# The second chunk of a tile's transposes behind the step's first job instead of in front of it

## Chip, core and metric

The kernel runs on 1 core of one Trainium2 chip. The metric is device time in microseconds (us) of one execution, given as the median of several. Lower is better.

## What is computed

x is 2 x 1024 tokens of 256 numbers. The result is x + attention(norm(x)) + ffn(norm(x)).

```python
x = L0_attn_x
xn = _layernorm(x, axis=-1)
x = x + _L0_attn_ref(xn, Wq, bq, Wk, bk, Wv, bv, Wo, bo) + _L0_ffn_ref(xn, gate, up, down, ...)

# attention: b, t = 2, 1024; 16 heads of 128
q = (x @ Wq + bq).reshape(b, h, t, dh)
k = (x @ Wk + bk).reshape(b, t, h, dh).transpose(0, 2, 3, 1)
v = (x @ Wv + bv).reshape(b, t, h, dh).transpose(0, 2, 1, 3)
logits = jnp.einsum('bhtd,bhds->bhts', q, k) * scale
weights = jax.nn.softmax(logits + mask, axis=-1)        # causal mask
out = jnp.einsum('bhts,bhsd->bhtd', weights, v)
return out.transpose(0, 2, 1, 3).reshape(b, t, h * dh) @ Wo + bo
```

The feed-forward part (4-bit weights, a gelu gate) runs in the first 320 us of the kernel and isn't touched.

## The kernel before

There are 2 x 16 = 32 heads, numbered 0 to 31, one after the other. Each has 8 query tiles of 128 rows, so the attention is a sequence of 256 steps; step s = 8h + i is position i of head h. In heads 0 to 30 tile i stands at position i; head 31 takes its tiles in the order 4, 6, 7, 5, 2, 3, 1, 0. Tile t looks at t + 1 key blocks of 128.

Every product is computed in three fp32r pieces (`split_matmul`, L41, L42, L43), each value being split into a high and a low part. A tile passes through all engines:

- PE: `scores(s)`, queries times keys, into one of two pairs of PSUM banks S.
- DVE L963: negative maximum and copy to `probs`. ACT L507: exp. POOL L737, L740: the reciprocal of the row sum and the product with it; this ends in `probs_done`.
- PE: three steps later (LAG = 3), `transposes(s - LAG)`: t + 1 transposes of 128 x 128 (L1169). Tiles 4 to 7 have two chunks: key blocks 0 to 3, and the rest (1, 2, 3 or 4 blocks). The chunks of all tiles go in turn into two PSUM banks T. The first transpose of a chunk waits on `pt_lo_done` until the chunk before the last one has been copied out of its bank.
- ACT L493 (`pt_high`): copy of a chunk out of its bank into `pt_hi`. DVE L880 (`pt_low`): the remainder into `pt_lo`, which frees the bank.
- PE: `with_v`, products with the values.

Between these stand jobs of six or twelve products: K (keys of a head, `project_k`), V (values, `project_v`) and O (a quarter of the output product, `output`). A table by position says which job stands where: FIRST is between the transposes and the scores of the step, EARLY behind the scores, LATE behind `with_v`. A job waits for `job_lo_done` of the job before it, since they share the bank M. A K or V job is copied out by ACT (L472, L475) and then by DVE (L835, L839), an O job by DVE alone (L846).

```python
EVEN = {0: {EARLY: "K0"}, 1: {FIRST: "K1"}, 2: {EARLY: "O0a"}, 3: {LATE: "O0b"}, 4: {EARLY: "V0", LATE: "V1"},
        6: {FIRST: "O1a"}, 7: {FIRST: "O1b"}}
ODD = {0: {EARLY: "V2"}, 1: {FIRST: "K1"}, 2: {EARLY: "V3"}, 3: {LATE: "O0a"}, 4: {EARLY: "O0b", LATE: "K0"},
       6: {FIRST: "O1a"}, 7: {FIRST: "O1b"}}
```

Head 0 has no first job; head 1 is as ODD from position 1 on; head 30 is as EVEN, with O1a and O1b early and one more early K job at position 5; head 31 has first jobs at positions 1 (V3), 2 (O0a), 4 (O1a) and 5 (O1b). In heads 7, 15 and 23 steps of the Q projection (`q_step`) stand behind positions 1, 2, 4 and 5 as well.

The order of each engine is the order of its code. ACT's step is: `pt_high(s - LAG)` for both chunks, then `evacuate` of the first job, then exp, then the early job. DVE's step is: `pt_low` of both chunks, the first job's copy, the maximum of step s, the early job's copy.

Of the kernel before, what the change touches and what calls it, by code (L numbers as in the profile page):

```python
# [38 lines left out]
def split_matmul(nc, out, w_hi, w_lo, m_hi, m_lo, start, stop):  # L39

    nc.tensor.matmul(out, w_hi, m_hi, start=start, stop=False)  # L41
    nc.tensor.matmul(out, w_hi, m_lo, start=False, stop=False)  # L42
    return nc.tensor.matmul(out, w_lo, m_hi, start=False, stop=stop)  # L43


def wait(eng, sem, count):

    if count > 0:
        eng.wait_ge(sem, count)
# [6 lines left out]
def attention(nc, sh, d, out):  # L56
# [8 lines left out]
    LAG = 3  # L65
# [15 lines left out]
    with ExitStack() as c:  # L81
# [103 lines left out]
        def job_of(h, i, where):  # L185

            name = JOBS[h].get(i, {}).get(where)
            if name is None:
                return None
            if name[0] == "K":  # L190
                return ("K", h if name == "K1" else h + 1, int(name[1]))
            if name[0] == "V":
                return ("V", h // 2, int(name[1]))
            return ("O", h - 1, int(name[1]), "ab".index(name[2]))
# [10 lines left out]
        banks_of = lambda i: 1 if i < QT else 2  # L205
# [9 lines left out]
        def k_of(h, half):  # L215

            if half and h + 1 == NH:
                return [t[:, 0:N] for t in wq_space]
            return [t[:] for t in (k_right if half else (k_even, k_odd)[h % 2])]

        def q_of(h, half):

            if half and h + 1 == NH:
                return [t[:, N:2 * N] for t in wq_space]
            return [t[:, half, :] for t in (q_hi, q_lo)]
# [57 lines left out]
        def freed_by(job):  # L283

            if job in (END[1], END[3], ("K", 0, 1), ("V", 0, 1)):
                return 0
            return max((nth[other] for other in ORDER[:nth[job] - 1] if (other in elsewhere) == (job in elsewhere)), default=0)
# [705 lines left out]
        def _(pe):  # L993
            def bank_free(*turn):

                if place[turn] < 2:
                    return
                kind, a, b = TURNS[place[turn] - 2]
                if kind == "S":
                    pe.wait_ge(max_done, step_of(a, b) + 1)  # L1000
                elif kind == "F":
                    pe.wait_ge(hid_done, a + 1)
                else:
                    pe.wait_ge(q_even_done, a * GROUP + b + 1)
                    pe.wait_ge(q_odd_done, a * GROUP + b + 1)
# [44 lines left out]
            def down(p, b):  # L1050

                pe.wait_ge(hid_lo_done, 2 * p + 2)
                if p == 0:
                    pe.wait_ge(xt_lo_done, KC * TC)
                if p:
                    pe.wait_ge(acc_done, half_no(p - 1, b))
                for t in range(2):
                    cols = slice((2 * b + t) * P, (2 * b + t + 1) * P)
                    for k in (2 * p, 2 * p + 1):
                        slot = slot_of(chunk_j(k))  # L1060
                        last = split_matmul(nc, D[b][:, t * DM:(t + 1) * DM], hid_hi[:, k % 4, cols], hid_lo[:, k % 4, cols],
                                            w_hi[:, slot, 4 * P:W6], w_lo[:, slot, 4 * P:W6], k == 2 * p, k == 2 * p + 1)
                last.then_inc(down_done, 1)
# [38 lines left out]
            def run(job):  # L1102
                if job is None:
                    return
                wait(pe, job_lo_done, freed_by(job))
                last = {"K": project_k, "V": project_v, "O": output}[job[0]](*job[1:])
                if job != END[3]:
                    last.then_inc(job_done, 1)

            def q_step(o, u):  # L1110
                bank_free("Q", o, u)
                cols = slice(o * N, (o + 1) * N)
                for v in range(2):
                    n = o * HEADS + 2 * u + v
                    pe.wait_ge(wq_lo_done, n + 1)
                    for ch in range(KC):
                        last = split_matmul(nc, bank_of("Q", o, u)[:, v, :], wq_hi[:, n % LOADS, ch, :],
                                            wq_lo[:, n % LOADS, ch, :], xn_hi[:, ch, cols], xn_lo[:, ch, cols],
                                            ch == 0, ch == KC - 1)
                    last.then_inc(qp_done, 1)  # L1120
# [17 lines left out]
            def scores(s):  # L1138
                h, i = divmod(s, TILES)
                tile = tile_of(h, i)  # L1140
                bank_free("S", h, tile)
                if i == 0:
                    pe.wait_ge(job_lo_done, nth[("K", h, 0)])
                if tile == QT:
                    pe.wait_ge(job_lo_done, nth[("K", h, 1)])
                half, cols = tile // QT, slice(tile % QT * P, (tile % QT + 1) * P)
                if i == 0 or half != tile_of(h, i - 1) // QT:
                    pe.wait_ge(q_lo_done, q_count(h, half))
                hi, lo = q_of(h, half)
                for bank in range(half + 1):  # L1150
                    width = min(N, (tile + 1) * P - bank * N)
                    keys_hi, keys_lo = k_of(h, bank)
                    last = split_matmul(nc, bank_of("S", h, tile)[:, bank, 0:width], hi[:, cols], lo[:, cols],
                                        keys_hi[:, 0:width], keys_lo[:, 0:width], True, True)
                last.then_inc(scores_done, 1)

            def transposes(s):
                i = tile_at(s)
                pe.wait_ge(probs_done, s + 1)
                if s == 0:  # L1160
                    pe.wait_ge(acc_done, STEPS)
                if s == 1:
                    pe.wait_ge(job_lo_done, nth[("K", 0, 1)])
                for ch in range(banks_of(i)):
                    at = chunk_no(s, ch)
                    wait(pe, pt_lo_done, at - 1)
                    for n in range(min(QT, i + 1 - ch * QT)):
                        b = ch * QT + n
                        last = nc.tensor.transpose(T[at % 2][:, n * P:(n + 1) * P], probs(s, i)[:, b * P:(b + 1) * P],  # L1169
                                                   ident[:])  # L1170
                    last.then_inc(pt_done, 1)

            def with_v(h, m, side):

                last_tile = QT * m + QT - 1
                blocks = range(QT) if side == "left" else range(QT, TILES)
                pe.wait_ge(pt_lo_done, chunk_no(step_of(h, last_tile), blocks[-1] // QT) + 1)
                pe.wait_ge(job_lo_done, nth[("V", h // 2, blocks[-1] // 2)])
                if blocks[0] == 0:
                    wait(pe, o_lo_done, 2 * h + m if h + 1 < NH else 2 * h)  # L1180
                for b in blocks:
                    first = max(b - QT * m, 0) * P
                    last = split_matmul(nc, O[:, first:], v_hi[:, h % 2, b, :], v_lo[:, h % 2, b, :],
                                        pt_keys(pt_hi, m, b), pt_keys(pt_lo, m, b), b == 0, b == last_tile)
                if blocks[-1] == last_tile:
                    last.then_inc(pv_done, 1)
# [50 lines left out]
            for s in range(NH * TILES):  # L1237
                h, i = divmod(s, TILES)
                if s >= LAG:
                    transposes(s - LAG)  # L1240
                run(job_of(h, i, FIRST))
                scores(s)
                run(job_of(h, i, EARLY))
                if s == 1:
                    down(*halves_at(STEPS + 1))
                    down(*halves_at(STEPS + 2))
                for m, side in pv_at(h, i):
                    with_v(h - 1, m, side)
                run(job_of(h, i, LATE))
                for u in q_steps(h, i):  # L1250
                    q_step(h // GROUP + 1, u)

            end = NH * TILES
            with_v(NH - 1, 1, "left")
            transposes(end - 3)
            transposes(end - 2)
            with_v(NH - 1, 1, "right")
            transposes(end - 1)
# [53 lines left out]
```

## Time and profile before

| | before |
|---|---|
| median of 3 runs | 1227.37 us (1227.34 to 1227.98) |
| the profiled execution | 1227.42 us, of which the trace spans 1225.6 us |
| PE busy | 1213.0 us (99%), 7556 products |
| DVE busy | 855.2 us (70%) |
| ACT busy | 746.7 us (61%) |
| POOL busy | 747.3 us (61%) |
| PE clock granted | 1.0 over the span |

A product's row starts when the product before it has been streamed, and its own duration reaches over the start of the next; the distance between two starts is what a product costs in the stream. PEld is PE's loading of stationary operands, which runs ahead of the products.

### The profile page before, as it was taken

Reading aid. Unit: us, or ns where it says so; the run is one execution under the profiler, and the core shown is the slowest. Engines: PE = TensorE matmul, PEld = TensorE weight load, DVE = VectorE, ACT = ScalarE, POOL = GpSimd, SP = SyncE. Lnnn points to the kernel's source line nnn. Section 1 sums busy time; section 2 is a strip of 40 time slices with the busy share of each in tenths; the row PEclk is TensorE's granted clock in tenths of the full one; section 3 lists DMA queues with packets and bytes.
Section 4 is the critical chain, followed back from the end, with each engine's and each line's share of the span. In section 5 each row is a group of like instructions: output and inputs, shape, how many; then the busy total and the mean of one; then the engine's idle time right before and its main releaser. Section 6 shows DMA issues by size and latency. Waiting matters only on the chain.

```text
span 1225.6 us, 20582 instructions
## 1 busy us (share of the span) xinstructions
PE 1213.0 (99%) x7556; PEld 1077.0 (88%) x7556; DVE 855.2 (70%) x1675; ACT 746.7 (61%) x1548; POOL 747.3 (61%) x797
## 2 busy tenths in 40 slices
PE   9999999999999999999999999999999999999998
PEld 7788888888889899889899988889898889899987
DVE  6777777776676766766677666676767766677675
ACT  5644444444576766666666765676667666666664
POOL 7346455543677666536767772677667536767764
PEclk9999999999999999999999999999999999999999
DMA  7100000000000000110000012010000100000001
GB/s 170 32 7 14 14 12 8 27 1 9 14 13 14 14 21 27 44 31 14 27 14 14 14 31 65 14 48 14 14 27 23 56 1 13 27 14 14 14 6 35
DMA packets 57347, 29.86 MB, mean 24 GB/s; under 512 B 16289, under 2 KB 57249, under 8 KB 57249
## 3 DMA queue, kind: packets, MB, share of 16 engines
q1 hardware_dynamic: 55888, 27.49, 8.0%
q8 instruction: 62, 1.02, 0.3%
q10 hardware_dynamic: 1360, 1.06, 0.3%
q14 instruction: 37, 0.30, 0.1%
HBM read 26.44 MB, written 2.10 MB: 23 GB/s over the span
## 4 chain that ended last, share of the span: by engine, by line
PE 93%; DVE 3%; ACT 2%; DMA 1%; POOL 1%; issue 1%; SPq 0%; DVEq 0%; ACTq 0%; POOLq 0%
PE ps L41 27%; PE ps L43 27%; PE ps L42 27%; PE ps L1169 10%; PE ps L1031 1%; DMA wq_in<-in_wq 1%; DVE pt_lo L880 1%; ACT q_all L415 0%; DVE acc L846 0%; DVE probs L963 0%; DMA acc<-in_x 0%; ACT wq_hi L405 0%; ACT pt_hi L493 0%; POOL wq_lo L624 0%; SPq L325 0%
## 5 line engine op out<-in xcount | busy, mean ns | idle before, releaser
L740 POOL TENSOR_TENSOR probs<-probs,inv_sum 128x128 f32<-128x128 f32 (+7 forms) x256 | 293.6, 1147 | 20.1
L737 POOL TENSOR_TENSOR inv_sum<-row_sum,minus_one 128x1 f32<-128x1 f32 x256 | 140.5, 549 | 219.5 <-ACT probs L507 218.4
L507 ACT ACTIVATE probs<-probs,neg_max 128x128 f32<-128x128 f32 (+7 forms) x256 | 198.8, 777 | 92.9 <-DVE neg_max L963 90.4
L493 ACT ACTIVATE pt_hi<-ps 128x512 fp32r<-128x512 f32 (+3 forms) x384 | 173.5, 488 | 91.4 <-PE ps L1169 88.7
L880 DVE TENSOR_TENSOR pt_lo<-ps,pt_hi 128x512 fp32r<-128x512 f32 (+3 forms) x384 | 200.6, 550 | 15.9 <-ACT pt_hi L493 15.8
L963 DVE CUSTOM_DVE_ANT_0 probs<-ps,mask_row 128x128 f32<-128x128 f32 (+7 forms) x256 | 191.8, 749 | 6.6
L1169 PE MATMUL ps<-ident,probs 128*128 128x128 f32 x1152 | 168.7, 274 | 3.2 <-DVE pt_lo L880 1.8
L721 POOL TENSOR_TENSOR hid_lo<-act_buf,hid_hi 128x512 fp32r<-128x512 f32 x64 | 82.8, 1294 | 139.5 <-ACT hid_hi L447 139.5
L1169 PEld LDWEIGHTS ps<-ident,probs 128*128 128x128 f32 x1152 | 133.8, 141 | 16.1 <-issue 5.2
L42 PE MATMUL ps<-pt_lo,v_hi 128*128 128x512 f32 (+3 forms) x386 | 133.0, 344 | 0.0
L43 PE MATMUL ps<-pt_hi,v_lo 128*128 128x512 f32 (+3 forms) x386 | 132.9, 344 | 0.0
L41 PE MATMUL ps<-pt_hi,v_hi 128*128 128x512 f32 (+3 forms) x386 | 130.2, 337 | 0.0
L846 DVE TENSOR_TENSOR acc<-ps,acc 128x512 f32<-128x512 f32 x127 | 86.9, 685 | 57.9 <-PE ps L43 57.9
L624 POOL TENSOR_TENSOR q_lo<-q_all,q_hi 128x512 fp32r<-128x512 f32 x63 | 81.3, 1291 | 73.5 <-ACT q_hi L484 73.5
L548 ACT ACTIVATE act_buf<-ps 128x512 f32<-128x512 f32 x64 | 38.2, 597 | 132.2 <-PE ps L43 132.2
L41 PE MATMUL ps<-xn_hi,w_hi 128*128 128x512 f32 x256 | 102.9, 402 | 1.1 <-DVE act_buf L933 1.1
L42 PE MATMUL ps<-xn_lo,w_hi 128*128 128x512 f32 x256 | 101.3, 396 | 0.0
L43 PE MATMUL ps<-xn_hi,w_lo 128*128 128x512 f32 x256 | 101.0, 394 | 0.0
L888 DVE SCALAR_TENSOR_TENSOR o_lo<-ps,bv,o_hi 128x512 fp32r<-128x512 f32 x63 | 47.3, 751 | 74.6 <-ACT o_hi L500 74.6
L839 DVE TENSOR_TENSOR v_lo<-ps,v_hi 128x512 fp32r<-128x512 f32 x64 | 44.2, 691 | 59.2 <-ACT v_hi L475 59.2
L41 PEld LDWEIGHTS ps<-pt_hi,v_hi 128*128 128x128 f32 x386 | 72.5, 188 | 8.8
L42 PEld LDWEIGHTS ps<-pt_lo,v_hi 128*128 128x128 f32 x386 | 72.6, 188 | 8.7
(154 smaller groups left out, 3372.4 us busy)
## 6 DMA issues: line engine op xcount, KB each, us to landing
wq_in<-in_wq SPq DMA_DIRECT2D x63, 128.0 KB, 2.3
kv_in<-in_wk SPq DMA_DIRECT2D x16, 256.0 KB, 2.6
wo_in<-in_wo SPq DMA_DIRECT2D x32, 128.0 KB, 2.0
kv_in<-in_wv SPq DMA_DIRECT2D x32, 128.0 KB, 2.4
out<-acc SPq DMA_DIRECT2D x7, 256.0 KB, 2.8
acc<-in_x SPq DMA_DIRECT2D x2, 512.0 KB, 5.3
raw<-in_gate SPq DMA_DIRECT2D x16, 64.0 KB, 1.8
raw<-in_up SPq DMA_DIRECT2D x16, 64.0 KB, 2.1
```

The costliest lines, as they stand in the source:

```text
L41: nc.tensor.matmul(out, w_hi, m_hi, start=start, stop=False)
L42: nc.tensor.matmul(out, w_hi, m_lo, start=False, stop=False)
L43: return nc.tensor.matmul(out, w_lo, m_hi, start=False, stop=stop)
L493: nc.scalar.activation(pt_blocks(pt_hi, i, ch), T[at % 2][:, 0:blocks * P].rearrange("p (a b) -> p a b", b=P), ACT.Copy).then_inc(pt_hi_do ...
L507: nc.scalar.activation(row, row, ACT.Exp, bias=neg_max[:, s % 16:s % 16 + 1], scale=-1.0, accum_out=row_sum[:, s % 16:s % 16 + 1]).then_in ...
L721: nc.gpsimd.tensor_tensor(hid_lo[:, k % 4, :], act_buf[:, k % 4, :], hid_hi[:, k % 4, :].bitcast(F32), ALU.subtract).then_inc(hid_lo_done, 1)
L737: nc.gpsimd.tensor_tensor(inv_sum[:, at], row_sum[:, at], minus_one[:], ALU.pow).then_inc(inv_done, 1)
L740: nc.gpsimd.tensor_tensor(row, row, inv_sum[:, at].to_broadcast([P, (tile_of(h, i) + 1) * P]), ALU.mult).then_inc(probs_done, 1)
L846: ins = nc.vector.tensor_tensor(sums, bank_for(job), sums, ALU.add)
L880: nc.vector.tensor_tensor(pt_blocks(pt_lo, i, ch), T[at % 2][:, 0:blocks * P].rearrange("p (a b) -> p a b", b=P), pt_blocks(pt_hi, i, ch). ...
L963: nc.vector.tensor_tensor_reduce(probs(s, tile), flat(bank_of("S", h, tile))[:, 0:width], mask_row[:, SEQ - width:SEQ], -1.0, -MASKED, ALU ...
L1169: last = nc.tensor.transpose(T[at % 2][:, n * P:(n + 1) * P], probs(s, i)[:, b * P:(b + 1) * P], ident[:])
```

## The change

`transposes` takes the chunks to do. In every step the first chunk stands where both stood; the second now stands behind the first job and in front of the scores. Nothing else is edited: the code of ACT, DVE, POOL and the DMA queues is the same.

```diff
-            def transposes(s):
+            def transposes(s, chunks=(0, 1)):
                 i = tile_at(s)
                 pe.wait_ge(probs_done, s + 1)
...
-                for ch in range(banks_of(i)):
+                for ch in chunks[:banks_of(i)] if 0 in chunks else chunks[:banks_of(i) - 1]:
...
                 if s >= LAG:
-                    transposes(s - LAG)
+                    transposes(s - LAG, (0,))
                 run(job_of(h, i, FIRST))
+                if s >= LAG:
+                    transposes(s - LAG, (1,))
                 scores(s)
```

The order moves where a step has a first job and the tile of three steps ago has two chunks: position 1 of heads 1 to 30 (tile 6, 4 + 3 transposes around K1), position 7 of heads 1 to 29 (tile 4, 4 + 1 around O1b), and positions 1, 2, 4 and 5 of head 31: 63 places. The wait for `probs_done` is now written twice in each of 253 steps.

On PE, position 1 of head 2, before (the names with `kv_` are job K1, those with `k_` and `q_` the scores):

```order
L1169 MATMUL ps<-ident,probs 128x128 x7
L41 MATMUL ps<-xn_hi,kv_hi 128x512
L42 MATMUL ps<-xn_lo,kv_hi 128x512
L43 MATMUL ps<-xn_hi,kv_lo 128x512
L41 MATMUL ps<-xn_hi,kv_hi 128x512
L42 MATMUL ps<-xn_lo,kv_hi 128x512
L43 MATMUL ps<-xn_hi,kv_lo 128x512
L41 MATMUL ps<-k_hi_even,q_hi 128x256
```

and with the change:

```order
L1169 MATMUL ps<-ident,probs 128x128 x4
L41 MATMUL ps<-xn_hi,kv_hi 128x512
L42 MATMUL ps<-xn_lo,kv_hi 128x512
L43 MATMUL ps<-xn_hi,kv_lo 128x512
L41 MATMUL ps<-xn_hi,kv_hi 128x512
L42 MATMUL ps<-xn_lo,kv_hi 128x512
L43 MATMUL ps<-xn_hi,kv_lo 128x512
L1169 MATMUL ps<-ident,probs 128x128 x3
L41 MATMUL ps<-k_hi_even,q_hi 128x256
```

Three of the seven transposes of tile 6 have moved behind the six products of K1.

On ACT, positions 1 and 2 with the change (`k_hi_right` is the copy of K1):

```order
L493 ACTIVATE pt_hi<-ps 128x4x128
L493 ACTIVATE pt_hi<-ps 128x3x128
L472 ACTIVATE k_hi_right<-ps,bk 128x512
L493 ACTIVATE pt_hi<-ps 128x4x128 x2
L507 ACTIVATE probs,row_sum<-probs,neg_max 128x256
```

Nothing has moved here: the copy of the three-block chunk stands ahead of the copy of K1, as before, and so it does on DVE. At position 7 one of the five transposes of tile 4 moves in the same way, behind the six products of O1b.

## Rows read from the trace of the kernel before

**Rows 1.** The page, busy time and share of the span by engine

```profile
PE 1213.0 (99%) x7556; PEld 1077.0 (88%) x7556; DVE 855.2 (70%) x1675; ACT 746.7 (61%) x1548; POOL 747.3 (61%) x797
```

**Rows 2.** Timeline of DVE, head 10: start us, us, instruction [idle before <-releaser]

```profile
600.85 0.55 DVE L880 TENSOR_TENSOR pt_lo<-ps,pt_hi 128x384 fp32r<-128x384 f32 x1
601.76 0.75 DVE L835 SCALAR_TENSOR_TENSOR k_lo_right<-ps,bk,k_hi_right 128x512 fp32r<-128x512 f32 x1 [0.36 <-ACT k_hi_right L472]
602.77 0.69 DVE L880 TENSOR_TENSOR pt_lo<-ps,pt_hi 128x512 fp32r<-128x512 f32 x1
```

**Rows 3.** Timeline of PEld, head 10, positions 2 and 3

```profile
601.52 0.14 PEld L1169 LDWEIGHTS ps<-ident,probs 128*128 128x128 f32 x1
602.57 0.19 PEld L41 LDWEIGHTS ps<-wo_hi,o_hi 128*128 128x128 f32 x1
603.57 0.14 PEld L1169 LDWEIGHTS ps<-ident,probs 128*128 128x128 f32 x1 [0.24 <-issue]
```

**Rows 4.** PEld, first load of the position-2 job: heads 2 and 30

```profile
373.20 0.19 PEld L41 LDWEIGHTS ps<-wo_hi,o_hi 128*128 128x128 f32 x1
...
1164.60 0.19 PEld L41 LDWEIGHTS ps<-wo_hi,o_hi 128*128 128x128 f32 x1
```

**Rows 5.** Timeline of ACT, head 10, positions 1 and 2

```profile
599.93 0.49 ACT L493 ACTIVATE pt_hi<-ps 128x384 fp32r<-128x384 f32 x1
601.04 0.69 ACT L472 ACTIVATE k_hi_right<-ps,bk 128x512 fp32r<-128x512 f32 x1 [0.62 <-PE ps L43]
601.83 1.08 ACT L493 ACTIVATE pt_hi<-ps 128x512 fp32r<-128x512 f32 x2
```

**Rows 6.** Timeline of PE, head 10, positions 1 to 3

```profile
598.66 0.95 PE L1169 MATMUL ps<-ident,probs 128*128 128x128 f32 x7
599.37 0.47 PE L41 MATMUL ps<-xn_hi,kv_hi 128*128 128x512 f32 x1
...
600.84 0.28 PE L41 MATMUL ps<-k_hi_even,q_hi 128*128 128x256 f32 x1
...
601.19 1.03 PE L1169 MATMUL ps<-ident,probs 128*128 128x128 f32 x8
601.98 0.42 PE L41 MATMUL ps<-k_hi_even,q_hi 128*128 128x384 f32 x1
...
602.59 0.36 PE L41 MATMUL ps<-wo_hi,o_hi 128*128 128x256 f32 x1
602.79 0.28 PE L42 MATMUL ps<-wo_lo,o_hi 128*128 128x256 f32 x1
...
603.60 0.30 PE L1169 MATMUL ps<-ident,probs 128*128 128x128 f32 x1
```

**Rows 7.** Copy of O1a on DVE, then first load of O1b: heads 9, 10

```profile
591.49 0.68 DVE L846 TENSOR_TENSOR acc<-ps,acc 128x512 f32<-128x512 f32 x1
592.22 0.19 PEld L41 LDWEIGHTS ps<-wo_hi,o_hi 128*128 128x128 f32 x1
...
617.27 0.68 DVE L846 TENSOR_TENSOR acc<-ps,acc 128x512 f32<-128x512 f32 x1
618.09 0.19 PEld L41 LDWEIGHTS ps<-wo_hi,o_hi 128*128 128x128 f32 x1
```

**Rows 8.** Head 9 into 10: tile 5's probs on POOL, its first transpose's load

```profile
592.73 1.47 POOL L740 TENSOR_TENSOR probs<-probs,inv_sum 128x768 f32<-128x768 f32 x1
594.25 0.14 PEld L1169 LDWEIGHTS ps<-ident,probs 128*128 128x128 f32 x1
```

**Rows 9.** Head 31: loads that end PE's waits, and what DVE did

```profile
1195.06 0.68 DVE L846 TENSOR_TENSOR acc<-ps,acc 128x512 f32<-128x512 f32 x1
1195.79 0.19 PEld L41 LDWEIGHTS ps<-wo_hi,o_hi 128*128 128x128 f32 x1 [0.50 <-DVE acc L846]
```

**Rows 10.** Timeline of PE, head 10, position 4

```profile
607.90 0.38 PE L1169 MATMUL ps<-ident,probs 128*128 128x128 f32 x2
608.04 0.48 PE L41 MATMUL ps<-k_hi_even,q_hi 128*128 128x512 f32 x1
```

## The prediction

> **What bounds the kernel.** I read the page's shares first: PE is busy 99% of the span [rows 1]. So nothing that makes another engine faster can gain much, but anything that lets PE wait is lost one for one. The question is then how much spare time the waits of PE have at the places where the order moves. For that I took the timelines of all engines at positions 1 and 2 of a head, and there the reader should see three things.
>
> First, the bank of a chunk. The second chunk of tile 7 (position 2) goes into the bank of the second chunk of tile 6 (position 1). DVE has emptied that bank at 600.85 + 0.55 = 601.40 [rows 2], and PE starts the load for the next chunk at 601.52 [rows 3]. PE didn't wait there, but the smallest distance of such a load behind such a copy that I see is 0.12: the transpose at 603.57 does wait, idle for 0.24, for the copy 602.77 + 0.69 = 603.46 [rows 2, 3]. So the margin is about nothing.
>
> Second, the bank of the jobs. The load of the job at position 2 starts at 602.57, 0.06 behind the end of K1's copy, 601.76 + 0.75 = 602.51 [rows 2, 3]. It is held by this copy already. The same 0.06 (0.053 unrounded) stands in 26 heads, from the load at 373.20 in head 2 to that at 1164.60 in head 30 [rows 4]; heads 7, 15 and 23 aren't among them, for two steps of the Q projection stand between.
>
> Third, ACT waits 0.62 for PE before it copies K1, at 601.04 [rows 5]. Its copy of the three-block chunk is long done (599.93 + 0.49). With the change this copy can't start until K1 is done, and K1's own copy still stands behind it.
>
> **Position 1, worked out on head 10.** PE does the same 4 + 6 + 3 instructions, so it loses nothing by itself. Transposes start 0.11 apart and the next product 0.03 behind the last one: eight take 601.98 - 601.19 = 0.79 [rows 6]. K1 takes 600.84 - 599.37 = 1.47 with a few hundredths for the passage from transposes to products; I take 1.45. The three transposes begin at 598.66 + 0.36 + 1.45 = 600.47, the last of them at 600.69. ACT begins a copy 0.31 behind the start of the last transpose: in tile 7 that is the fourth, at 601.52, and the copy is at 601.83 [rows 5, 6]. So the three-block copy runs on ACT from 601.00 to 601.49, on DVE (0.03 later, as in 601.73 to 601.76 for K1 [rows 2, 5]) from 601.52 to 602.07, and the load for tile 7's second chunk can start at 602.07 + 0.12 = 602.19. Before it was at 601.52: **0.67 later**, and everything behind it on PE with it.
>
> The other chain is shorter. K1's copy on ACT starts 0.37 behind that of the chunk (two copies overlap by 0.1: the two at 601.83 take 1.08 together [rows 5]), at 601.37 instead of 601.04, so DVE is through at 602.84 and the job may load at 602.90. The job's own place is now 602.59 + 0.67 = 603.26, so this wait is covered. It disappears. Of the 0.20 from the job's first product to its second, 602.59 to 602.79 [rows 6], I count 0.03 as waiting, the rest as the passage between two kinds of product; it can't be more than 0.08, the distance between the two products less the 0.12 at which such products follow. Left at the job's start: 0.64.
>
> In the 15 even heads from 2 to 30 the job is O0a, of 0.7 to 0.8 us, and behind it the single transpose of tile 0 waited for the copy of tile 7's first chunk. That copy is held on DVE by K1's copy and moves by 0.33 only, to 603.79, so its load is possible at 603.91; O0a ends for PE at about 604.01. The old wait is hidden by the new one, and the transpose moves from 603.60 to 604.01: 0.41, less 0.02 that a waiting transpose costs more. **15 x 0.39 = 5.9 us.**
>
> In the odd heads 3 to 29 without 7, 15, 23 the job is V3, 1.47 us, and nothing waited behind it. **11 x 0.64 = 7.0 us.** Heads 7, 15, 23: nothing, the Q steps (over 5 us) cover all. Head 1 has its DVE later than the others by 0.2 to 0.3 already, so it takes about 0.2.
>
> **Position 7.** O1b waits for DVE's addition of O1a. In odd heads this binds: the addition ends at 592.17 and O1b loads at 592.22 [rows 7]. O1b can't go earlier, and the one transpose behind it costs 0.12 (0.04 and the 0.08 of the passage). Then tile 5's first transpose waits for POOL: its probs end at 592.73 + 1.47 = 594.20, its load is at 594.25 [rows 8], where some 0.08 is waiting; this hides the 0.08. I take 0.05 in 12 odd heads and 0.12 in 7, 15, 23. In even heads the addition ends at 617.95 and O1b loads at 618.09 [rows 7], so 0.09 of the 0.12 comes back: 0.03 in 14 heads. Sum 0.6 + 0.4 + 0.4 = **1.4 us**. From the same rows it is at least 0 and at most 29 x 0.12 = 3.5. The copies of this one block (ACT, DVE) fall in time that is idle or ahead of a maximum not yet ready.
>
> **Head 31.** Four first jobs follow each other closely, and O jobs wait for the addition of the job before: O0b loads at 1195.79, 0.05 behind the addition 1195.06 + 0.68, after 0.50 of idle [rows 9]. With the change the copies of a four-block chunk, which now is transposed behind O0a, stand ahead of that addition: last transpose at 1194.4, ACT 1194.7 to 1195.3, DVE to 1196.0, the addition to 1196.6, O0b at 1196.6: +0.8. At positions 4 and 5 the same pattern comes again; worked down it gives about 1.1 more, by the same durations. I take **1.9 us**, between 0.3 (position 1 alone) and 3.
>
> **The repeated waits** for `probs_done` are in 253 steps, and the flag is up each time. A group of scores with three waits (position 4) starts 0.03 behind its last transpose (607.90 + 0.11, then 608.04 [rows 10]), the same 0.03 as one with a single wait at position 2 [rows 6]. I cost them at nothing: these equal distances show no price. The two bounds are 0 and the 0.06 by which a load with two waits (0.12) starts later than one whose only late flag it was (0.06) [rows 2, 3], that is 253 x 0.06 = 15 us.
>
> The Trainium skill (Advanced Engine Details and Errata, Network/Comms) gives 50 to 100 ns for reading a semaphore from a sequencer on TRN2. If each repeated wait cost that on PE's path, an estimate from that page alone would be 13 to 25 us on top, and the trace speaks against it with its equal 0.03.
>
> **Sum.** 5.9 + 7.0 + 0.2 + 1.4 + 1.9 = 16.4. Against the profiled execution's 1227.42 (span 1225.6 and 1.8 around it) that is 1243.8; the median of the runs is 1227.37, the same within 0.1.
>
> **Rivals.**
>
> A. Only the jobs' bank counts, because the chunk's bank is free earlier than I think (the three blocks copied sooner, say). Then each of 26 heads loses the 0.33 of K1's copy: 8.6 + 0.2 + 1.4 + 1.9 = 12.1, so 1239.5. For it: this chain is the plain one. Against it: 602.07 is 0.6 behind the old start of the load.
>
> B. The repeated waits cost too: 1243.8 + 15 = 1259 at most. Against it: the equal distances of [rows 6, 10].
>
> C. Faster. K1 now ends 0.35 earlier on PE. If its copy could use that, that is if ACT and DVE had the three-block chunk out of the way before K1 ended, the 0.03 at the job and the wait of 0.22 at tile 0 would go: 26 x 0.03 + 15 x 0.22 = 4.1, so 1223.3. It decides at the point where the three-block copy on DVE is done before 601.40 instead of 602.07. The order on PE puts those transposes behind K1, so it is 0.67 short.
>
> D. No change: all of it falls into slack, 1227.4. It would need some 0.6 us between 601.40 and 601.52.
>
> E. The waits add up: tile 0's transpose in even heads still waits 0.24 behind the shifted job, if DVE's chain moves as much as PE's. 15 x 0.25 more: 1247.6.
>
> **The numbers.** My forecast (chunk's bank, both chains) 0.68, A 0.14, E 0.08, B 0.03, C 0.03, D 0.04. Slower in all but C and D: 0.93. About 0.2%, 2.5 us, is what a measurement of this kernel can tell from no change: faster 0.03, same 0.04, slower 0.93. The range takes A from below, with position 7 and head 31 at their lower ends (12.1 - 1.4 - 0.9: 1237), and E above (1247.6), rounded to 1237 to 1248. Outside it lie B, C and D, together 0.10, and the mishaps of my sum.
>
> **What would show it.** In the changed profile: at position 2 the load of the fifth of the eight transposes starts about 0.12 behind the end of the three-block `pt_lo`, with an idle of 0.5 to 0.7 ahead of it, in 26 heads, and DVE `pt_lo` becomes the releaser of some 14 to 16 us of PE's idle time. ACT waits for L1169 before the three-block copy and not before K1's. The jobs at position 2 no longer load 0.06 behind K1's copy; tile 0's transpose waits no more. Per pair of heads the period grows by about 1.1 us. I am wrong if the eight transposes of tile 7 still take 0.79 (then A or D), or if the scores start more than 0.05 behind their transposes in steps without a job (then B).

## The result, and the profile after

| | before | with the change |
|---|---|---|
| median | 1227.57 us (4 runs, 1227.34 to 1227.98) | 1245.36 us (4 runs, 1244.29 to 1245.54) |
| ratio to before | | 1.0143, 95% interval 1.0131 to 1.0154 |
| the profiled execution | 1227.42 us, span 1225.6 | 1245.5 us, span 1243.7 |

The change costs 17.8 us. The forecast was 1243.8 us, 16.4 more than the profiled execution before, with a range of 1237 to 1248.

The page's busy times, against [rows 1]:

```profile
PE 1218.0 (98%) x7556; PEld 1078.5 (87%) x7556; DVE 858.6 (69%) x1675; ACT 744.7 (60%) x1548; POOL 747.6 (60%) x797
```

PE does the same 7556 products. The span of the trace has grown by 18.1 us, PE's busy time by 5.0 only (a product's row reaches beyond the start of the next product, so it covers the beginning of a wait behind it). The other 13.1 us are idle time, and the table of waits says what ended it (who waited and for whom: us in total, times, longest). With the change:

```profile
ACT pt_hi L493 <- PE ps L1169: 133.6, 210, 2.6
...
DVE pt_lo L880 <- ACT pt_hi L493: 36.5, 55, 2.9
...
PE ps L1169 <- DVE pt_lo L880: 14.6, 30, 1.0
```

and before:

```profile
ACT pt_hi L493 <- PE ps L1169: 88.7, 122, 2.6
...
ACT k_hi_right L472 <- PE ps L43: 17.9, 29, 0.6
...
DVE pt_lo L880 <- ACT pt_hi L493: 15.8, 23, 2.9
...
PE ps L1169 <- DVE pt_lo L880: 1.8, 3, 0.9
```

The chain reads from bottom to top: PE's transposes wait for DVE's `pt_lo` (1.8 has become 14.6), DVE for ACT's `pt_hi` (15.8, now 36.5), ACT for PE's transposes (88.7, now 133.6). ACT's 29 waits for K1 are gone, since it now finds K1 done behind the late chunk.

Position 1 and 2 of head 10 with the change; everything stands 4.82 us later than in the rows before. PEld, against [rows 3]:

```profile
607.06 0.42 PEld L1169 LDWEIGHTS ps<-ident,probs 128*128 128x128 f32 x4 [0.68 <-issue]
...
607.91 0.19 PEld L41 LDWEIGHTS ps<-wo_hi,o_hi 128*128 128x128 f32 x1
...
608.77 0.14 PEld L1169 LDWEIGHTS ps<-ident,probs 128*128 128x128 f32 x1
```

ACT, against [rows 5]:

```profile
605.86 0.49 ACT L493 ACTIVATE pt_hi<-ps 128x384 fp32r<-128x384 f32 x1 [1.01 <-PE ps L1169]
606.25 0.68 ACT L472 ACTIVATE k_hi_right<-ps,bk 128x512 fp32r<-128x512 f32 x1
```

DVE, against [rows 2]:

```profile
606.38 0.56 DVE L880 TENSOR_TENSOR pt_lo<-ps,pt_hi 128x384 fp32r<-128x384 f32 x1 [0.64 <-ACT pt_hi L493]
606.96 0.75 DVE L835 SCALAR_TENSOR_TENSOR k_lo_right<-ps,bk,k_hi_right 128x512 fp32r<-128x512 f32 x1
...
607.97 0.69 DVE L880 TENSOR_TENSOR pt_lo<-ps,pt_hi 128x512 fp32r<-128x512 f32 x1
```

PE, against [rows 6]:

```profile
605.34 0.49 PE L1169 MATMUL ps<-ident,probs 128*128 128x128 f32 x3
...
606.02 0.60 PE L1169 MATMUL ps<-ident,probs 128*128 128x128 f32 x4
...
607.48 0.42 PE L41 MATMUL ps<-k_hi_even,q_hi 128*128 128x384 f32 x1
...
608.80 0.30 PE L1169 MATMUL ps<-ident,probs 128*128 128x128 f32 x1
608.93 0.47 PE L41 MATMUL ps<-k_hi_even,q_hi 128*128 128x512 f32 x1
```

The three transposes start at 605.34; ACT has waited 1.01 for them; DVE ends at 606.94; the load for tile 7's second chunk follows 0.12 later, at 607.06, after 0.68 of idle. The eight transposes that took 0.79 [rows 6] now take 1.46 (606.02 to 607.48) with the hole in their middle. The job's load at 607.91 is 0.20 behind the end of K1's copy (607.71), so that wait is covered. The transpose of tile 0 at 608.80 no longer shows idle time in the table, but its load at 608.77 is again 0.11 behind DVE's copy of tile 7's first chunk (607.97 + 0.69 = 608.66), the distance at which a load follows the copy it waits for. And the scores at 608.93 start 0.13 behind this transpose, where the kernel before had 0.05 (603.60 to 603.65): between them now stands the repeated wait for `probs_done`. Both come back below.

To add the losses up I take the start of a step's first transpose in both traces and look at how the difference grows, position by position:

| place | forecast | trace |
|---|---|---|
| positions 1 to 3, even heads 2 to 30 | 15 x 0.39 = 5.9 | 15 x 0.45 = 6.75 |
| positions 1 to 3, odd heads 3 to 29 without 7, 15, 23 | 11 x 0.64 = 7.0 | 11 x 0.60 = 6.6 |
| head 1, positions 1 to 3 | 0.2 | 0.23 |
| heads 7, 15, 23, positions 1 to 3 | 0 | 0.0 |
| position 7 (to position 0 of the next head) | 1.4 | 2.1: even heads 0.04, odd 0.10 to 0.12 |
| head 31 | 1.9 | 2.3 |
| ahead of the attention, and the rest | 0 | 0.1 |
| together | 16.4 | 18.1 |

### The profile page after: what moved, and what is told of

Its sections match the earlier page's. It is cut to its first block, busy times and chain, and to the rows that moved or that the text cites. A ratio compares the mean times of both kernels' runs of the same rounds, so it can differ in the third digit from the quotient of the medians.

```text
span 1243.7 us, 20823 instructions
## 1 busy us (share of the span) xinstructions
PE 1218.0 (98%) x7556; PEld 1078.5 (87%) x7556; DVE 858.6 (69%) x1675; ACT 744.7 (60%) x1548; POOL 747.6 (60%) x797
## 4 chain that ended last, share of the span: by engine, by line
PE 90%; DVE 4%; ACT 3%; issue 1%; DMA 1%; POOL 0%; SPq 0%; DVEq 0%; ACTq 0%; POOLq 0%
PE ps L41 27%; PE ps L43 27%; PE ps L42 27%; PE ps L1169 9%; DVE pt_lo L880 2%; ACT pt_hi L493 1%; PE ps L1031 1%; DMA wq_in<-in_wq 1%; DVE acc L846 0%; ACT q_all L415 0%; DMA acc<-in_x 0%; DVE probs L963 0%; POOL wq_lo L624 0%; ACT wq_hi L405 0%; SPq L325 0%
## 5 line engine op out<-in xcount | busy, mean ns | idle before, releaser
L493 ACT ACTIVATE pt_hi<-ps 128x512 fp32r<-128x512 f32 (+3 forms) x384 | 183.8, 489 | 133.6 <-PE ps L1169 133.6
L880 DVE TENSOR_TENSOR pt_lo<-ps,pt_hi 128x512 fp32r<-128x512 f32 (+3 forms) x384 | 204.0, 552 | 36.7 <-ACT pt_hi L493 36.5
L1169 PE MATMUL ps<-ident,probs 128*128 128x128 f32 x1152 | 184.2, 274 | 14.9 <-DVE pt_lo L880 14.6
```

The source lines that it names most:

```text
L493: nc.scalar.activation(pt_blocks(pt_hi, i, ch), T[at % 2][:, 0:blocks * P].rearrange("p (a b) -> p a b", b=P), ACT.Copy).then_inc(pt_hi_do ...
L880: nc.vector.tensor_tensor(pt_blocks(pt_lo, i, ch), T[at % 2][:, 0:blocks * P].rearrange("p (a b) -> p a b", b=P), pt_blocks(pt_hi, i, ch). ...
```

## The experiments

Each is the kernel before, or the change, with one edit. Growth per head is read as in the table above; ratios are to the kernel before, run in the same job.

**p1_only: position 1 alone**

```diff
+                behind = i == 1 and h + 1 < NH
                 if s >= LAG:
-                    transposes(s - LAG, (0,))
+                    transposes(s - LAG, (0,) if behind else (0, 1))
                 run(job_of(h, i, FIRST))
-                if s >= LAG:
+                if s >= LAG and behind:
                     transposes(s - LAG, (1,))
```

> Only position 1 of heads 1 to 30 has its second chunk behind K1; position 7 and head 31 are as before. Theory (the bank of tile 6's second chunk comes free late): the load for tile 7's second chunk waits 0.68 in 26 heads, no repeated waits matter, 13.3 to 13.8 us slower than before, 1241.1. Rival (only the jobs' bank counts): +9. Rival (half of the loss is from position 7 and head 31): +8 or less.

1239.18 us, ratio 1.0098 (1.0085 to 1.0112): +12.0, below the 13.3 to 13.8 expected. The trace has 0.38 per even and 0.53 per odd head at positions 1 to 3 and nothing of note anywhere else. Position 1 is two thirds of the loss, but each head lost 0.07 less than with the whole change. In the odd heads the load for tile 7's second chunk explains it; in head 10 it is

```profile
605.30 0.14 PEld L1169 LDWEIGHTS ps<-ident,probs 128*128 128x128 f32 x1 [0.62 <-DVE pt_lo L880]
```

Here head 10's first transpose of tile 6 is at 601.78, so the load comes 3.52 behind it, with the change 607.06 - 603.48 = 3.58; DVE's copy ends 3.47 behind it in both. A load with one wait follows the copy by 0.05, one with two waits (the change writes the wait for `probs_done` again in front of the one for the bank) by 0.12. The odd heads have the same distances. In the even heads this 0.07 doesn't reach the next tile: the transpose of tile 0 starts 5.32 behind that of tile 6 in both runs, and the two part only behind it, where the scores of position 3 follow after 0.06 here and after 0.13 with the change.

**p7_only: position 7 alone** (the same edit with `behind = i == 7 and h + 1 < NH`)

> Only position 7 of heads 1 to 29 has its second chunk behind O1b. Theory: 0.1 in each odd head, 0.03 in each even one, 1.6 to 2.2 us slower than before, 1229.5. Rival (PE loses only what it waits, and the odd heads' place is covered by the probs wait of tile 5): +0.3 to 0.8.

1229.11 us, ratio 1.0012 (1.0003 to 1.0021): +1.9. The trace has 0.03 to 0.04 in each even head and 0.11 in each odd one, those with Q steps among them: 2.2 together, of which the odd heads give 0.6 back at positions 3 and 4 (0.03 at each).

**last_only: head 31 alone** (the same edit with `behind = h + 1 == NH`)

> Only head 31 has its second chunks behind its four first jobs. Theory: the additions of O0a and O1a wait for the copies of the chunk, so O0b and O1b load later: 2.0 to 2.5 us slower, 1229.9. Rival (head 31 waits for POOL's probs anyway, so it is hidden): below +0.5.

1229.69 us, ratio 1.0020 (1.0011 to 1.0029): +2.5. The trace has 2.28 within head 31. The whole change shows what it is made of; DVE and PEld at position 2 of head 31:

```profile
1211.33 0.69 DVE L880 TENSOR_TENSOR pt_lo<-ps,pt_hi 128x512 fp32r<-128x512 f32 x1 [0.53 <-ACT pt_hi L493]
1211.93 0.68 DVE L846 TENSOR_TENSOR acc<-ps,acc 128x512 f32<-128x512 f32 x1
```

```profile
1209.24 0.19 PEld L41 LDWEIGHTS ps<-wo_hi,o_hi 128*128 128x128 f32 x1 [0.37 <-DVE v_lo L839]
1212.67 0.19 PEld L41 LDWEIGHTS ps<-wo_hi,o_hi 128*128 128x128 f32 x1 [1.05 <-DVE acc L846]
```

The addition of O0a (1211.93) stands behind the copy of a chunk that is transposed only after O0a, and O0b loads 0.06 behind its end, after 1.05 of idle against 0.50 [rows 9]. O0a itself waits 0.37 for V3's copy, which is held in the same way.

**wait_twice and wait_once: the repeated waits**

wait_twice is the kernel before with

```diff
                 run(job_of(h, i, FIRST))
+                if s >= LAG:
+                    pe.wait_ge(probs_done, s - LAG + 1)
                 scores(s)
```

> The kernel before with one more wait for probs_done ahead of each of 253 groups of scores, nothing else. Theory (a wait on a flag that is up costs PE's products nothing): within 0.5 us of before. Rival (each costs 0.06 on PE's path): up to +15 us.

1228.04 us, ratio 1.0006 (0.9997 to 1.0015): +0.8, not clear of nothing by its runs. Its trace is clearer: no position of any odd head moves by more than 0.04, the mean is nothing, and each even head loses 0.07 at position 3. There the transpose of tile 0 waits, and the scores behind it now start 0.13 after it, not 0.05 as before (603.60 to 603.65):

```profile
603.82 0.30 PE L1169 MATMUL ps<-ident,probs 128*128 128x128 f32 x1
603.95 0.47 PE L41 MATMUL ps<-k_hi_even,q_hi 128*128 128x512 f32 x1
```

wait_once is the whole change with the wait for `probs_done` in the first call only:

```diff
                 i = tile_at(s)
-                pe.wait_ge(probs_done, s + 1)
+                if 0 in chunks:
+                    pe.wait_ge(probs_done, s + 1)
```

(and the two waits of steps 0 and 1 likewise).

> The change with the wait for probs_done written once only, order of products the same. Theory: within 0.5 us of the change, 1245.4. Rival (repeated waits are a part of the loss): 1233 to 1243.

1242.9 us, ratio 1.0131 (1.0115 to 1.0146): +16.0, where the whole change had 17.8. That is the rival's range and not the theory's. The intervals overlap; the traces again don't: 0.38 and 0.53 per even and odd head at positions 1 to 3, where the change has 0.45 and 0.60, and nearly equal elsewhere. So the repeated wait costs 0.07 in each of 26 heads, 1.8 us, and nothing that shows in the other steps. In the 11 odd heads it does so at tile 7's second chunk, in the 15 even heads behind tile 0's transpose, as in wait_twice; at either place PE is waiting for a copy. The three parts measured alone, none of which repeats waits in steps without a move, give 12.0 + 1.9 + 2.5 = 16.4, close to wait_once's 16.0.

**copies_follow: ACT and DVE copy K1 first, as PE makes it**

Position 1 alone moved, and on ACT (on DVE likewise):

```diff
+                swap = i == 1 and 0 < h < NH - 1
                 if s >= LAG:
-                    pt_high(s - LAG)
+                    pt_high(s - LAG, (0,) if swap else (0, 1))
                 evacuate(job_of(h, i, FIRST))
+                if swap:
+                    pt_high(s - LAG, (1,))
```

> Position 1 alone moved, and ACT and DVE now copy K1 ahead of the three-block chunk, as PE makes them. Theory (the chunk's bank is what PE waits for): K1's copies (0.60 on ACT, 0.67 on DVE) now stand ahead of the chunk's, pt_lo of the three blocks ends some 0.54 later than with position 1 alone, 26 x 0.54 = 14 us more: about 1255. Rival (the jobs' bank is what PE waits for, K1's copy being held behind the chunk's): the loss of position 1 goes away and PE's old waits too, 1223 to 1229.

1251.18 us, ratio 1.0198 (1.0184 to 1.0212): +24.3, twice the loss of position 1 alone. The load waits still longer for `pt_lo` (4.05 us behind the first transpose of tile 6 instead of 3.52):

```profile
609.51 0.20 PEld L1175 LDWEIGHTS ps<-ident,probs 128*128 128x128 f32 x2 [1.15 <-DVE pt_lo L883]
```

Here K1's copy does use the earlier K1 (in head 10 DVE is through with it 3.53 behind the first transpose of tile 6, before the change 3.85), and it gains nothing, since the chunk behind it is the later one. My 0.54 per head was 0.44 to 0.51, and the total was put at 27.6 for 24.3, half of the difference because position 1 alone had been put too high.

**tile7_late: the chunk that waits goes behind the scores**

Position 1 alone moved, and at position 2 of heads 1 to 30:

```diff
+                late = i == 2 and 0 < h < NH - 1
...
-                    transposes(s - LAG, (0,) if behind else (0, 1))
+                    transposes(s - LAG, (0,) if behind or late else (0, 1))
...
                 scores(s)
+                if late:
+                    transposes(s - LAG, (1,))
                 run(job_of(h, i, EARLY))
```

> Position 1 alone moved, and at position 2 of heads 1 to 30 the second chunk of tile 7 is transposed behind the scores of that step, 0.6 later. Theory: that covers the wait for the chunk's bank but for 0.1 or less, and what is left is the wait of the job for K1's copy, which starts 0.33 later: 26 x 0.34 + 0.4, about 9 us slower than before, 1236.8. Rival (K1's copy is no limit): 1228 to 1230. Rival (the chunk's bank isn't what PE waits for): 1241 as with position 1 alone.

1237.18 us, ratio 1.0084 (1.0070 to 1.0097): +10.3. The table of waits now has the jobs' bank in the place of the chunk's:

```profile
PEld ps L41 <- DVE k_lo_right L835: 7.6, 26, 0.3
...
PE ps L1169 <- DVE pt_lo L880: 1.8, 3, 0.9
```

Even and odd heads both lose 0.39. So the second chain (K1's copy, held behind the chunk's and waited for by the next job) is there, as rival A had it. In the odd heads the longer first chain hides it (0.53 in p1_only). In the even heads tile 0's transpose waits for a copy that DVE makes behind K1's, and moving tile 7's chunk away gave nothing (0.38 in p1_only, 0.39 here): there the second chain is the one that counts. With the first chain covered 26 x 0.39 = 10.1 us are left.

**half_k1: the three transposes in the middle of K1**

The kernel before, with the second chunk at position 1 between the third and the fourth product of K1:

```diff
                                         xn_lo[:, ch, cols], ch == 0, ch == KC - 1)
+                    if between is not None and ch == 0:
+                        transposes(between, (1,))
```

> The kernel before, with the second chunk at position 1 of heads 1 to 30 between the third and the fourth product of K1, 0.7 earlier than the change puts it. Theory (the loss is lateness beyond a slack): the last transpose is read by ACT from about 600.3 on in head 10's times, when ACT would have come to it at 599.9, DVE is through at 601.4 as before, so nothing waits: 0 to +1 us, 1227.6 to 1228.6. Rival (splitting the seven transposes or changing between kinds of product costs PE by itself): +3 to +6 us. Rival (any move is paid in proportion): half of 13.5, +7.

1226.66 us, ratio 0.9998 (0.9990 to 1.0007): no difference. PE's waits for `pt_lo` are those of before:

```profile
PE ps L1175 <- DVE pt_lo L880: 1.8, 3, 0.9
```

Splitting the seven transposes and changing between kinds of product costs PE nothing that can be seen. The transposes are 0.7 us later than before here, and twice that in the change. The first 0.7 us is free, but only just: DVE is through with the three blocks 0.03 later than before. The loss lies in the second 0.7.

**max_behind and vw_ahead: taking away the wait at tile 0**

In the kernel before, the transpose of tile 0 in even heads waits about 0.22 for DVE's copy of tile 7's first chunk. On DVE I put this copy ahead of the maximum of position 1:

```diff
-                    for ch in range(banks_of(tile_at(s - LAG))):
+                    for ch in range(1 if ahead and i == 2 else 0, banks_of(tile_at(s - LAG))):
                         pt_low(s - LAG, ch)
                 evacuate(job_of(h, i, FIRST))
+                if ahead and i == 1:
+                    pt_low(s - LAG + 1, 0)
```

(`ahead` is true in the even heads 2 to 30.)

> The kernel before, with one edit on DVE: in the even heads 2 to 30 the low part of tile 7's first chunk is made ahead of the maximum of position 1 instead of behind it. Theory (the 0.22 that tile 0's transpose waits in these heads ends with that copy, which DVE could make from 602.46 on instead of 602.77 in head 10's times): the transpose waits no more, but the scores behind it then wait for the later maximum; 0.1 to 0.2 less in 15 heads, 1.5 to 3 us faster, 1225.5. Rival (this maximum is as late as the copy was, so one wait takes the place of the other): within 0.5 us of before. Rival (exp and POOL get the tile later and its transposes wait): slower by 1 to 3 us.

1230.96 us, ratio 1.0030 (1.0018 to 1.0042): +3.3. None of the three expectations: 0.08 per even head was gained at positions 1 to 3, and 0.34 lost at position 4, for a new releaser:

```profile
PE ps L41 <- POOL vw_lo L624: 2.5, 15, 0.2
```

The later maximum makes exp later, and so the division of tile 1 on POOL by 0.63. Behind it and tile 2's division in POOL's queue stands the low part of the V weights, which job V0 at position 4 needs. In vw_ahead that part is made ahead of tile 2's division:

```diff
+                if i == 2 and h % 2 == 0 and h:
+                    vw_low(h // 2)
                 pool.wait_ge(exp_done, s + 1)
...
-                    if h % 2 == 0 and h:
-                        vw_low(h // 2)
```

> The same edit on DVE as in max_behind, and on POOL the low part of the V weights (vw_lo) is made ahead of tile 2's division at position 2 instead of behind it, in the even heads from 2 on. Theory (max_behind lost because job V0 at position 4 waited for vw_lo, 0.34 in each of 15 heads, and gained 0.08 at tile 0): with vw_lo done 2 us earlier only the gain is left, 1.2 us faster than before, 1226.2 to 1226.8. Rival (tile 2's division, now later by 1.3, is waited for by its transposes or by those of a later tile): 1229 to 1240. Rival (the loss came from elsewhere): 1231 as max_behind.

1226.18 us, ratio 0.9987 (0.9978 to 0.9996): 1.6 us faster than before, in the direction and about the size expected. Its trace gains 0.08 in each even head at positions 1 to 3 and loses nothing behind. It beats both kernels, by less than what a measurement of this kernel tells surely.

## Why the prediction was right

**The mechanism.** The step that carried the sum was that the order on PE had moved and the orders on ACT and DVE had not. The trace has each link as it was put: the load waits for the end of the three-block copy and follows it by 0.12; I had it 3.53 behind tile 6's first transpose and it is 3.58, since DVE's copy ends 0.06 later than worked out (K1 and the passages around it took 0.05 more than the 1.45 and 0.36 I used). p1_only and half_k1 show that this place, and lateness in it, is the loss; copies_follow shows that an earlier copy of K1 doesn't make up for a later one of the chunk. But this load is what sets the loss in the odd heads only.

**Both chains.** That K1's copy is the shorter chain at the job was right, and tile7_late made it visible at 0.39 per head, where I had put 0.33 to 0.34. Behind the job, in even heads, it is the longer one.

**Even heads** were put at 0.39 and are 0.45, and the 0.39 owes something to luck. I had the job's end let the transpose of tile 0 go at 5.35 us after tile 6's first transpose, with DVE's copy ready for it at 5.25, and called the old wait hidden. The means of the 15 even heads, in the same measure, show it nearly gone (0.21 before, 0.01 with the change), but it is still DVE's copy that comes last. The last column is what PE would allow, worked out as the start of the job's last product and the 0.12 at which the transpose follows it in copies_follow, where it doesn't wait:

| run | DVE's copy ends | transpose of tile 0 | PE would allow |
|---|---|---|---|
| before | 4.79 | 4.93 | 4.72 |
| p1_only | 5.18 | 5.32 | 5.25 |
| tile7_late | 5.18 | 5.32 | 5.10 |
| with the change | 5.18 | 5.32 | 5.31 |

The job's end moves by 0.2 between the last three runs and the transpose doesn't: its load is 0.12 behind DVE's copy in all of them. What sets the 0.39 is therefore the copy of K1, held behind the chunk's, and behind it that of tile 7's first chunk, which is rival A's mechanism. I had this copy move by 0.33 and it moved by 0.39; I had the job let the transpose go at 5.35, and it does at 5.31. So the two changed places, and the later of them stayed where the sum had it.

The term that was mis-sized is the repeated wait, put at nothing: here it costs 0.07, between tile 0's transpose and the scores of position 3. The argument for nothing, equal distances behind transposes, was taken from places where PE doesn't wait, and holds only there. The sign that I had given for B, scores more than 0.05 behind their transposes in a step without a job in front of them, did show at this one place of the even heads (0.13). Why the wait costs something just there, no run shows.

**Odd heads** were put at 0.64 and are 0.60. The load moved by 0.70 on the mean, more than the 0.67 I had, but the transpose it serves by 0.64 only, since before the change the load ran 0.10 ahead of its transpose and now 0.03. Another 0.04 came back by the end of the step, where I had 0.03 at the job. In the 0.60 is the 0.07 of the second wait at tile 7's chunk; here I had counted it, having taken 0.12 and not 0.05 as the load's distance.

**Position 7** was put at 1.4 and is 2.1. In odd heads the 0.08 which the wait for tile 5's `probs` should have hidden wasn't: each pays 0.10 to 0.12, as heads 7, 15 and 23 do. My reading of [rows 8] was wrong. The load does wait for POOL there, but the transpose behind it doesn't. PE in the kernel before:

```profile
594.17 0.40 PE L43 MATMUL ps<-k_hi_right,q_lo 128*128 128x512 f32 x1
594.40 0.27 PE L1169 MATMUL ps<-ident,probs 128*128 128x128 f32 x1
```

The transpose starts 0.23 behind the last product of the scores, and so in all 12 heads; two products of these scores are the same 0.23 apart. The load, at 594.25, waited while that product was still streaming, and there was nothing to give back.

**Head 31** was put at 1.9 and is 2.3, by the mechanism given: 1.1 up to position 3, put at 0.8, and 1.2 behind it, put at 1.1.

**The rivals.** A is the second chain: not the bound in odd heads, but what sets the loss in even ones, where the first comes level with it in the change. B, in its full size of 15 us, is ruled out; 1.8 us of it are real. C needed the three-block copy done on DVE before 601.40 in the times before; it is done at 606.94 - 4.82 = 602.12. D is what half_k1 shows for half the lateness. E's further 0.25 at tile 0 isn't there. The Trainium skill's 50 to 100 ns for reading a semaphore (Advanced Engine Details and Errata, Network/Comms) agrees in size with the 0.07 where PE waits, but no run shows it in the steps where PE doesn't.

## What to carry to other kernels

When one engine's work is moved in an order that several engines follow, write down the others' queues at that place: a copy that stands first in its queue and is now fed last holds everything behind it. Count the slack in the trace first; here 0.7 us of lateness was free, and the next 0.7 us cost 0.4 to 0.6 us in each of 26 heads. And look at the whole chain behind a wait before calling it hidden: a wait can end at the forecast time for another reason than the forecast one. An engine that is idle for hundreds of us (POOL here) can still hold a single result that has no slack.

## What the runs showed that I hadn't expected

A wait on a flag that is up costs nothing in a stream that runs (wait_twice, odd heads: 0.00) and 0.07 where it stands beside a wait that really holds, whether in the same group (the change, tile 7's second chunk in odd heads) or in the next group behind it (tile 0 in even heads, in wait_twice and in the change). And the low part of the V weights on POOL, with POOL busy for 61% of the span, was only 0.3 us ahead of its need (in head 10 before the change it ended at 608.73, and job V0 loaded at 609.04): in max_behind it came 0.46 later, which cost 0.34 per head.
